# Turning gathered embedding rows with four plain float32 products instead of four transposes

## The reference

```python
e = jnp.stack([tbl_0[ids[:, 0]], ..., tbl_31[ids[:, 31]]], axis=1)     # 2048 x 32 x 64
p, q = e[:, ids_x, :], e[:, ids_y, :]                                  # 496 pairs of fields
pw = jnp.einsum('bpi,pij->bpj', p, w)
z = jnp.einsum('bpj,bpj->bp', pw, q)                                   # 2048 x 496
h = jnp.concatenate([z, dense_ctx], axis=1)                            # 2048 x 512
h = jnp.maximum(h @ W_top1 + b_top1, 0.0)
h = jnp.maximum(h @ W_top2 + b_top2, 0.0)
y = h @ W_top3
```

## Time and profile before

| | |
|---|---|
| median of 3 runs | 1130.65 us (1128.81 to 1131.58) |
| the profiled execution | 1127.72 us, of which the span of the engines is 1125.9 us |
| PE busy | 899.1 us, 80% of the span |
| DVE busy | 597.6 us, 53% |
| POOL busy | 483.4 us, 43% |
| ACT busy | 67.6 us, 6% |
| DMA | 28.05 MB, mean 25 GB/s |

### The profile page before, as it was taken

The page is one execution under the profiler, slowest core; times in us unless marked ns, Lnnn a source line. Parts: engine busy times, 40 slices in busy tenths (PEclk is TensorE's granted clock), DMA queues, the critical chain, the costliest instruction groups (busy, mean ns, idle before and its releaser), DMA issues.

```text
span 1125.9 us, 11138 instructions
## 1 busy us (share of the span) xinstructions
PE 899.1 (80%) x4592; PEld 308.5 (27%) x4592; DVE 597.6 (53%) x512; ACT 67.6 (6%) x109; POOL 483.4 (43%) x516
## 2 busy tenths in 40 slices
PE   0320259999967789999997599999996599999999
PEld 0100013333322223333332133333332133333333
DVE  0100037778734445667774345567863355578880
ACT  0000000000000000000000000000000000100001
POOL 6777546543266625435356625435356632000000
PEclk9985669999987889999998889999998889999999
DMA  9311101100011101000011101000011100000000
GB/s 325 97 27 26 21 15 24 20 17 13 10 20 22 23 11 19 15 15 18 12 19 23 23 10 20 16 14 19 12 19 24 23 9 11 1 1 1 1 1 0
DMA packets 19348, 28.05 MB, mean 25 GB/s; under 512 B 8913, under 2 KB 9681, under 8 KB 18513
## 3 DMA queue, kind: packets, MB, share of 16 engines
q0 software_dynamic: 16384, 16.81, 8.1%
q1 hardware_dynamic: 2914, 10.53, 2.6%
HBM read 27.30 MB, written 0.01 MB: 24 GB/s over the span
## 4 chain that ended last, share of the span: by engine, by line
PE 70%; another core or an unknown queue 19%; DVE 5%; issue 3%; ACT 1%; DMA 1%; POOL 1%; DVEq 0%; POOLq 0%
PE main_ps L240 37%; PE z_ps L254 21%; PE x_ps L287 6%; DVE prod L312 5%; PE x_ps L223 3%; PE main_ps L287 2%; PE main_ps L241 2%; ACT e_t L323 1%; POOL emb L187 1%; DMA emb<-in_tbl,idx 1%; PE z_ps L258 0%; DMA idx<-in_ids 0%; DVEq L114 0%; ACT ctx_y L342 0%
## 5 line engine op out<-in xcount | busy, mean ns | idle before, releaser
L312 DVE TENSOR_TENSOR prod<-main_ps,e_t 128x1024 f32<-128x1024 f32 x512 | 597.6, 1218 | 500.3 <-PE main_ps L241 258.3
L187 POOL DMA_INDIRECT emb<-in_tbl,idx x512 | 483.2, 944 | 453.5 <-PE x_ps L223 244.4
L240 PE MATMUL main_ps<-e_t,w_sb 64*128 64x512 f32 x1024 | 512.3, 632 | 189.8 <-DVE prod L312 83.2
L241 PE MATMUL main_ps<-e_t,w_sb 64*128 64x512 f32 x1024 | 512.4, 632 | 0.0
L240 PEld LDWEIGHTS main_ps<-e_t,w_sb 64*128 64x128 f32 x1024 | 181.4, 192 | 465.8 <-issue 258.0
L254 PE MATMUL z_ps<-prod,const_sb 128*32 128x512 f32 x2048 | 264.9, 638 | 0.3 <-DVE prod L312 0.3
L241 PEld LDWEIGHTS main_ps<-e_t,w_sb 64*128 64x128 f32 x1024 | 181.1, 192 | 0.0
L254 PEld LDWEIGHTS z_ps<-prod,const_sb 128*32 128x32 f32 x2048 | 55.7, 114 | 192.8 <-issue 136.4
L323 ACT ACTIVATE e_t<-x_ps 128x512 f32<-128x512 f32 x64 | 38.2, 597 | 681.7 <-PE x_ps L223 341.5
L223 PE MATMUL x_ps<-const_sb,emb 128*128 128x128 f32 x256 | 44.5, 299 | 34.3 <-DMA emb<-in_tbl,idx 31.7
L223 PEld LDWEIGHTS x_ps<-const_sb,emb 128*128 128x128 f32 x256 | 28.6, 148 | 89.8 <-issue 75.0
(11 more groups left out here) (10 smaller groups left out, 11.8 us busy)
## 6 DMA issues: line engine op xcount, KB each, us to landing
emb<-in_tbl,idx POOLq DMA_INDIRECT x512
w_sb<-in_w SPq DMA_DIRECT2D x5, 1280.0 KB
w_sb<-in_w SPq DMA_DIRECT2D x1, 1024.0 KB
w_sb<-in_w SPq DMA_DIRECT2D x1, 512.0 KB
w_sb<-in_w SPq DMA_DIRECT2D x1, 448.0 KB
w_sb<-in_w SPq DMA_DIRECT2D x1, 384.0 KB
w_sb<-in_w SPq DMA_DIRECT2D x1, 320.0 KB
w_sb<-in_w SPq DMA_DIRECT2D x1, 256.0 KB, 3.4
```

Of the source, the lines that this page charges most:

```text
L187: pool.indirect_dma_start(out=emb[:, n % G_SLOTS, s, odd * EMBED:(odd + 1) * EMBED], out_offset=None, in_=tables[f], in_offset=bass.Indire ...
L240: nc.tensor.matmul(main_ps[:, slot, :], w_sb[LOW, u, :], even[LOW, 0, :], start=True, stop=True)
L241: nc.tensor.matmul(main_ps[:, slot + 1, :], w_sb[UP, u, :], odd[UP, 0, :], start=True, stop=True)\
L312: nc.vector.tensor_tensor(prod[:, s:s + 2, :], main_ps[:, slot:slot + 2, :], e_q, ALU.mult)\
```

## The change

The call of `nc.tensor.transpose` in `transpose_duo` becomes a call of `nc.tensor.matmul` with the same three operands in the same places. The stationary operand is still the gathered rows, the moving one still the identity, and the target the same 128 columns of `x_ps`. The product of the rows, which the array takes as transposed, with the identity is the transposed block.

```diff
                 for s in range(SUBS):
-                    last = nc.tensor.transpose(x_ps[:, s * P:(s + 1) * P], emb[:, n % G_SLOTS, s, :], ident)
+                    last = nc.tensor.matmul(x_ps[:, s * P:(s + 1) * P], emb[:, n % G_SLOTS, s, :], ident, start=True, stop=True)
                 last.then_inc(transposed, 1)
```

## The result

The changed kernel takes 1149.84 us (median of 4 runs, 1141.95 to 1155.49) against 1130.70 us before (1128.81 to 1131.58). The ratio is 1.0167, with a 95% interval of 1.0105 to 1.0228: slower by 1.7%. The forecast was 1148 us in a range of 1134 to 1166. The profiled execution is the slowest of the four, 1155.49 us with a span of 1153.7 us; the runs of the kernel before lie within 3 us of one another, those of the changed one within 14.

What follows compares the result with a forecast made beforehand. PE bounds the stretches within tiles, POOL's gathers and the late signals behind them the tile starts. 36 turns x 0.49 us = 17.6 us on the median 1130.65 us gives 1148 us, range 1134 to 1166.

Steps and rivals of the forecast that it cites:

- The turn: Each turn on L223 costs PE 0.44 us more stream and 0.05 us first load, 0.49 us; later loads hidden.
- Fourfold by the rule on the transposing mode: Rival: a product costs four transposes, 1.37 us more a turn, 49 us over 36 turns, 1180 us; chance 0.05.
- The waits swallow it: Rival: PE's idle gaps in three PE-bound stretches absorb the cost; only 9 turns count, 4.4 us, 1135 us; chance 0.08.
- Held signals: While POOL streams gathers, PE's finished work is made known late (duo 34: 9.4 us), so added PE work there is free.
- 0.5 us moves no signal across the end of a group of gathers: Argument against the faster rival: signals that matter leave before the group of gathers ends or long after.
- Which turns are on the path: Turns in PE-bound stretches count, 36 x 0.49 = 17.6 us; those in the streams of gathers cost nothing.
- The 36 turns: Duos 7, 10 to 15, 23 to 32, 39 to 48, 55 to 63, taken as on the path, 0.49 us each.
- the 2 us and the 1 us: Signs of error: stretches between tiles change over 2 us each; duo 32's to duo 38's copy leaves 69.6 us by over one.
- the 28 turns: Turns in the streams of gathers, with duos 8 and 9, costed at nothing; were the cover gone, 14 us.
- The 0.87 us behind duo 9: Read as PE waiting for a signal its turn doesn't make, so that turn fell off the path.
- 1163 us: Upper end of the forecast's own range, 1141 to 1163: all turns on the path, 14 + 4 us more.
- The other side: Rival, faster: where tiles begin, POOL pauses and releases held signals earlier, 8 us won in each of three stretches, 1124 us; chance 0.04.

Runs made afterwards that it cites:

- e1: Kernel before with each transpose issued twice in a row, same operands and target; 928.42 us, ratio 1.0266.
- e4: Kernel before (transposes) with the gathers of tiles 1 to 3 left out; 905.45 us, ratio 1.0007.
- e0: Changed kernel once more, no edit, on a chip where no signal is held; 932.09 us against 904.13 us, ratio 1.0309.
- e11: Changed kernel (products) with three of ACT's copies in each later tile made to wait for gathers seven duos on; 1008.81 us.
- e10: Kernel before (transposes) with three of ACT's copies in each later tile made to wait for gathers seven duos on; 991.78 us.
- e9: Changed kernel (products) with a memset and a wait for its end on POOL behind every gather; 1230.15 us.
- e8: Kernel before (transposes) with a memset and a wait for its end on POOL behind every gather; 1229.61 us.
- e3: Kernel before with products only in the 28 turns that the sum left off the path; 914.57 us, ratio 1.0112.
- e12: Kernel before once more, no edit, on a chip that holds signals; 1129.89 us profiled, 1128.85 us for the 13 runs beside it.
- e2: Kernel before with products only in the 36 turns that the sum put on the path; 922.18 us, ratio 1.0197.

## Why the prediction was right or wrong

*The turn.* Right. 0.44 us of stream and 0.05 us of load were forecast, 0.50 us is measured, in every PE-bound stretch of every trace. e1 splits it: 0.44 us are the four more passes, 0.06 us the plain loads. The loads behind the first hide although 0.10 us beside 0.107 us left no margin; the spacing of the matmuls went from 0.109 to 0.112 us.

*Fourfold by the rule on the transposing mode.* Wrong: the trace has 512 matmuls of 275 ns for 256 of 273 ns. The Trainium skill's TensorE: Matmul & The Clock Gate, section Terms, gives a factor of 4; here it is 2 in records, and 1.08 to 0.58 us in the turn. The Trainium skill's Perfetto Trace Analysis, section Transposes, asks that transposes be written as such; what this is worth here is the 0.50 us a turn.

*The waits swallow it.* Wrong: 6.30 and 6.22 us of idle PE in the same stretch. Where nothing is held, the same nine turns take 149.3 us with transposes (e4) and 153.8 us with products (e0): the idle time is gone, and the price is the same 4.5 us. So the gaps are no cover. That they move along because the gathers start from the turn's own signal, as forecast, is consistent with this, not tested by itself.

*Held signals.* What I read of them holds where signals are held: the releases behind POOL's stream are in both profiles of the kernel before. They cover the products of duos 33 to 36: the copies of duos 34 and 36 stay in place to 0.1 us. At the start of tile 3 the copy of duo 50 stays too, and that of duo 52 is 0.6 us later. That a release of this kind covers turns is also shown by e11 against e10, and for waits on gathers by e9 against e8. What fails is the sentence that 0.5 us moves no signal across the end of a group of gathers: in the kernel before, duo 37's signal came out at 635.3 us, 0.2 us before POOL finished the group ahead of the gathers that wait for it, and in the changed one POOL had to wait 1.95 us for it.

*Which turns are on the path: the step that is not shown, and elsewhere fails.* The 36 turns rest on the held signals. On three of the four chips of the experiments nothing is held, 57 turns are on the path and the price is 28.0 us, 3.1%, not 1.6%. I took what one chip did for a property of the kernel; the 904 us of another chip lay far outside anything I allowed for. On a chip that holds, 13.4 us come from 27 turns as forecast. For the rest of the kernel I forecast 9 turns, 4.4 us. At the medians it is 19.1 - 13.4 = 5.7 us, which fits, but the interval of the ratio (12 to 26 us in all) allows anything from none to 12 us. In the profiled execution it is 14.4 us. The kernel before differs from itself there too: to duo 15 it needs 314.1 us in one profile and 317.4 us in the other, the changed one 319.0 us. The starts of tiles take 3.1 to 4.7 us longer than in either profile of it, and duo 38's copy comes 64.6 us behind duo 32's instead of 69.6 us: more than the 2 us and the 1 us that I had named as signs of being wrong. The timeline shows why a small shift can count there: duo 38's signal slipped through early, and PE was held for 5.9 us behind the next gathers instead. That the median comes within 2 us of the forecast is thus in part luck. Whether the 28 turns cost something by themselves on such a chip, as these three stretches suggest, stays open: e3, which would tell, ran only where nothing is held. Why some chips hold signals is open too.

Two readings of mine were loose. The 0.87 us behind duo 9 stand as "issue", time for which the profile shows no wait, so the row doesn't say that PE waited for a signal there. And 1163 us, the upper end of the forecast's own range, is 1145.3 + 18; against the median it is 1166.

*The other side.* The stream of gathers does break at another place, as this rival has it, but nothing is won: the last group of the tile start begins 68.2 us behind the first, against 69.6 us, and the 1.4 us gained came back as a longer wait. What a shifted pause does to the time was costed in one direction only, and with the wrong sign.

## What to carry to other kernels

Here a float32 transpose goes through the array once per block (256 records of 273 ns) and a float32 product with the identity twice (512 of 275 ns): count records, and take the time of one from the slope of duration over columns. Count what such a change adds per use on the engine, and only then ask which uses are covered. A cover that rests on a late signal, with no instruction or transfer to show for the delay, may be a thing of the chip; keep the sum without it as a case of its own.

## What was not expected of the hardware

- On the chip of e12, and in the first profiles, what PE has finished is made known up to 10 us late while POOL streams indirect DMAs (duo 36's turn ends at 615.2 us and its copy starts at 625.11), and in tile 0 only once every 11.2 us (in the first profile DVE's instructions start at 76.41, 87.61 and 98.81 us, and ACT idles 44.20 us). With it the same program takes 1129 instead of 904 us, a quarter more.
- The granted clock fell to 0.50 between 75.5 and 82.2 us in e4, with four transposes a turn, and stayed at 1.00 in e1, with eight. The two rows (as above: length, PE and PEld busy, and on to the clock):

```profile
75.50:82.20 6.70, 6.07 (x22) 1.59 (x24) 1.23 (x1) 0.58 (x1) 4.96 (x6) 0.50 0.14 25
```

```profile
75.50:82.20 6.70, 6.01 (x37) 2.20 (x37) 2.66 (x3) 0.60 (x1) 5.14 (x6) 1.00 0.13 26
```

  Duo 7's turn came at 87.4 us in e4 and 85.1 us in e1. e2, with four transposes in each of its first seven turns, fell there too, to 0.52, but e10, with four transposes a turn as well, kept its clock there and reached duo 7 at 84.8 us, so the longer turns are not the only thing that decides it. The Trainium skill's TensorE: Matmul & The Clock Gate, section Part 4: PE-mode transpose, says that transposes don't count as activity for the clock; that e1, with transposes where e0 has products, runs at 1.00 there as e0 does shows no such difference where other products lie around them.
